# Attention in pairs of row blocks: which pair of blocks each iteration's 16 units begin with

## The chip, the cores and the metric

The kernel runs on one core of a Trainium2 chip, as a single program. The metric is the device time of that core in microseconds: the median of three runs is 3832.74 (3829.89 to 3833.71). A profiled execution, from which the rows below are taken, took 3835.85, and its span from first to last instruction is 3833.9.

## The reference

One transformer layer in float32 on x of 4 x 1024 x 512: layer norm, causal attention with 4 groups of 4 heads of width 128 (one key and value head per group), layer norm and residual; then a mixture of experts (32 experts, 4 per token, and a shared one) in the same frame.

```python
q = jnp.einsum('bim,ghmd->bghid', x, w_aq)
k = jnp.einsum('bim,gmd->bgid', x, w_ak)
v = jnp.einsum('bim,gmd->bgid', x, w_av)
q = _rope(q); k = _rope(k)
s = jnp.einsum('bghid,bgjd->bghij', q * qk_mult, k * qk_mult)
s = s - INF_APPROX * (i < j)
p = jax.nn.softmax(s, axis=-1)
o = jnp.einsum('bghij,bgjd->bghid', p, v)
r = jnp.einsum('bghid,ghdm->bim', o, w_ao)
...
x = x + _layernorm(attn(_layernorm(x)))
x = x + _layernorm(ffn(_layernorm(x)))
```

## The kernel before

Attention is a loop of 16 iterations, one for each batch b and group g, and it is written by hand for each engine: every engine has its own list, and they meet at semaphores. Numbers are kept as a high and a low part (names end in h and l), so each product is three matmuls (`mm3`, L820 to L822). One iteration has these stages.

Projection (`project`, tiles t = 0 to 7 of 128 rows): TensorE writes q, k and v of a tile into S, ScalarE copies it out (L726), VectorE and GpSimd do the rotation, TensorE turns the tile (`transpose_tile`, L862 for q and L865 for k), ScalarE casts the high part (`hi_tile`, L718 and L720) and VectorE subtracts to get the low part (`lo_tile`, L527 and L530).

Attention proper: the 8 row tiles form 4 row blocks of two tiles. A unit is one row block ib and one head h. With two row tiles a = 0 and 1 it has score blocks of (2 ib + 1) x 128 and (2 ib + 2) x 128 columns: 128 and 256 for block 0, 384 and 512 for block 1, 640 and 768 for block 2, 896 and 1024 for block 3. A unit has ib + 1 pairs of key tiles. BLOCKS says which two row blocks alternate in the first eight units and which in the last eight; UNITS, PAIRS, PROJECT_AT, OUTPUTS, PROJECTED and FINAL follow from it (L54 to L105). The steps of unit u are: scores (`scores`, two units ahead, into S[:, a]; the last piece adds the mask, L893), row maximum on VectorE (`row_max`, L559), exponential on ScalarE (`exp`, L734, which also frees S), transposes of the probabilities (`transpose_pair`, L908, into one of two banks of TP), the high part on ScalarE (`hi_pair`, L742) and the low part on VectorE (`lo_pair`, L571), the value matmuls (`value_pair`, which for a unit's first pair also spreads the reciprocals, L916), then L788, L577, L424 and L426, which normalise and split the result on ScalarE, VectorE and GpSimd. TensorE's list for a unit is, pair by pair: the transposes of the next pair, a score block of unit u + 2 for each of the first two pairs (a unit of block 0 has only one pair, and its second score block comes behind that), the value matmuls of this pair.

A transposes-ahead order means that the transposes of the pair after this one are issued first. When the next pair belongs to the next unit, they wait for both of that unit's exponentials. In `scores`, the first four units also wait for the low parts of the tiles they use: units 0 and 1 for tile i = 2 ib + a, unit 2 on for tile 7.

Output projection (`out_project`, L943 on): the first four row tiles at the start of units 8 and 9 (PROJECT_AT), the other four at the end (PROJECT_LAST).

Side work (`beside`), fixed to unit numbers by tables at L66 to L74: two portions of other tokens' norms, residual sum, transposes and router logits. The first has its steps at units 0, 1, 2, 2, 3, 3, 4, 6, 8 (XN, XH, XT_AT and RS, RA and RN, RH, HT_AT, LG_AT), the second at 8, 9, 9, 10, 10, 11, 12, 14, 15. On ScalarE these are L748, L751, L761, L764, L755 and L758, on VectorE L611, L600, L616, L622 with L624 and L625, L629 and L604 on, on GpSimd L362 to L383, on TensorE L959 and L964. The upper half of S[:, 1] is their transposes' target, and the second score block three units on waits until it has been read. GpSimd splits the weights for the next iteration and the output projection at odd units, and at unit 12 in three of the iterations it starts the reload of xTh and xTl (L409).

Of the kernel before, what the change touches and what calls it, by code (L numbers as in the profile page):

```python
# [50 lines left out]

IB = 2
NIB = NT // IB
BLOCKS = [(a, NIB - 1 - a) for a in reversed(range(NIB // 2))]  # L54
UNITS = [(ib, h) for blocks in BLOCKS for h in range(H) for ib in blocks]
PAIRS = [(u, jp) for u, (ib, h) in enumerate(UNITS) for jp in range(ib + 1)]
NPAIR = len(PAIRS)
# [39 lines left out]

PROJECT_AT = {HALFU + n: [IB * BLOCKS[0][n] + a for a in range(IB)] for n in range(2)}
PROJECT_LAST = [IB * ib + a for ib in BLOCKS[1] for a in range(IB)]

# [2094 lines left out]
```

## Time and profile before

| | |
|---|---|
| median of three runs | 3832.74 us |
| profiled execution | 3835.85 us, span 3833.9 us |
| TensorE busy | 3427.0 us, 89% |
| VectorE busy | 2253.4 us, 59% |
| GpSimd busy | 1635.9 us, 43% |
| ScalarE busy | 1603.6 us, 42% |
| attention, 16 iterations | about 38 to 2580 us |

A row of the timeline has the start, the time, the engine (PE is TensorE, DVE VectorE, ACT ScalarE, POOL GpSimd), the line of the kernel, the operation, output <- input by name, the shapes, the number merged into the row and, in brackets, how long the engine was idle before it and who released it. Times of a matmul row overlap with the next row's, as matmuls are pipelined. The iteration that begins at 514.97 is the one read closely.

### The profile page before, as it was taken

Reading aid. Unit: us, or ns where it says so; the run is one execution under the profiler, and the core shown is the slowest. Engines: PE = TensorE matmul, PEld = TensorE weight load, DVE = VectorE, ACT = ScalarE, POOL = GpSimd, SP = SyncE. Lnnn points to the kernel's source line nnn. Section 1 sums busy time; section 2 is a strip of 40 time slices with the busy share of each in tenths; the row PEclk is TensorE's granted clock in tenths of the full one; section 3 lists DMA queues with packets and bytes.
Section 4 is the critical chain, followed back from the end, with each engine's and each line's share of the span. In section 5 each row is a group of like instructions: output and inputs, shape, how many; then the busy total and the mean of one; then the engine's idle time right before and its main releaser. Section 6 shows DMA issues by size and latency. Waiting matters only on the chain. (4 is left out here: it accounts for less than half of the span.)

```text
span 3833.9 us, 73808 instructions
## 1 busy us (share of the span) xinstructions
PE 3427.0 (89%) x20373; PEld 2903.6 (76%) x20375; DVE 2253.4 (59%) x4900; ACT 1603.6 (42%) x3576; POOL 1635.9 (43%) x2112
## 2 busy tenths in 40 slices
PE   6999999999999999999899998985898999999987
PEld 5788777887878878778777787874686777777766
DVE  6665665656556565565665656655664454444448
ACT  2543534435344353443534435443123454444443
POOL 3433334333343333433334333345422555555548
PEclk9999999999999999999999999996899999999989
DMA  2111112111021210111121101126333777767767
GB/s 82 59 31 40 40 34 100 62 35 48 26 62 34 101 51 25 60 34 35 51 97 55 39 29 51 35 69 229 96 108 102 172 181 159 192 156 180 170 140 277
DMA packets 231764, 339.78 MB, mean 89 GB/s; under 512 B 20304, under 2 KB 105552, under 8 KB 230640
## 3 DMA queue, kind: packets, MB, share of 16 engines
q1 hardware_dynamic: 198128, 244.43, 19.7%
q0 software_dynamic: 33280, 91.02, 11.3%
q8 instruction: 173, 2.83, 0.3%
q14 instruction: 183, 1.50, 0.1%
HBM read 225.00 MB, written 110.38 MB: 87 GB/s over the span
## 5 line engine op out<-in xcount | busy, mean ns | idle before, releaser
L571 DVE TENSOR_TENSOR ptl<-TP,pth 128x512 fp32r<-128x512 f32 (+1 forms) x640 | 406.4, 635 | 231.3 <-ACT pth L742 223.7
L820 PE MATMUL O<-pth,vh 128*128 128x256 f32 (+1 forms) x1280 | 401.1, 313 | 55.9 <-DVE ptl L571 55.9
L742 ACT CAST pth<-TP 128x512 fp32r<-128x512 f32 (+1 forms) x640 | 344.5, 547 | 217.6 <-PE TP L908 216.4
L559 DVE TENSOR_REDUCE negmax<-S 128x1 f32<-128x384 f32 (+7 forms) x512 | 379.4, 748 | 27.2 <-PE S L893 25.3
L820 PE MATMUL S<-kTh,qTh 128*128 128x512 f32 (+3 forms) x768 | 302.5, 394 | 87.2 <-ACT work L734 40.1
L822 PE MATMUL O<-pth,vl 128*128 128x256 f32 (+1 forms) x1280 | 359.3, 281 | 0.0
L821 PE MATMUL O<-ptl,vh 128*128 128x256 f32 (+1 forms) x1280 | 358.6, 280 | 0.0
L820 PE MATMUL S<-wph,xTh 128*128 128x512 f32 (+1 forms) x1024 | 354.2, 346 | 3.5 <-issue 1.7
L402 POOL TENSOR_TENSOR work<-work,cst 128x320 f32<-128x320 f32 x128 | 132.3, 1034 | 504.8 <-ACT work L726 504.8
L821 PE MATMUL S<-wpl,xTh 128*128 128x512 f32 (+1 forms) x1024 | 346.6, 338 | 0.0
L822 PE MATMUL S<-wph,xTl 128*128 128x512 f32 (+1 forms) x1024 | 345.3, 337 | 0.0
L734 ACT ACTIVATE prob<-S,negmax 128x768 f32<-128x768 f32 (+5 forms) x288 | 265.5, 922 | 178.8 <-DVE negmax L559 178.8
L1651 POOL DMA_INDIRECT acc_d<-yb,idy x144 | 229.3, 1592 | 255.5 <-ACT yb L1702 238.5
L726 ACT COPY work<-S 128x768 f32<-128x768 f32 x128 | 102.5, 801 | 541.8 <-PE S L822 437.0
L820 PEld LDWEIGHTS O<-pth,vh 128*128 128x128 f32 x1280 | 243.2, 190 | 80.9 <-DVE ptl L571 80.5
L908 PE MATMUL TP<-cst,prob 128*128 128x128 f32 x1776 | 275.6, 276 | 17.9 <-ACT prob L734 17.7
L822 PE MATMUL S<-kTh,qTl 128*128 128x512 f32 (+3 forms) x768 | 268.2, 349 | 0.0
L821 PE MATMUL S<-kTl,qTh 128*128 128x512 f32 (+3 forms) x768 | 267.2, 348 | 0.0
L734 ACT ACTIVATE work<-S,negmax 128x128 f32<-128x128 f32 (+1 forms) x224 | 115.2, 514 | 333.5 <-DVE negmax L559 333.5
L1017 PE MATMUL S<-weh,hTh 128*128 (+1 forms) x576 | 242.9, 422 | 2.7 <-DVE wel L1741 2.7
L1034 POOL DMA_INDIRECT xg<-h_d,idx x146 | 192.9, 1321 | 122.2 <-DVE hTl L1749 54.7
L821 PEld LDWEIGHTS O<-ptl,vh 128*128 128x128 f32 x1280 | 243.2, 190 | 0.0
(319 smaller groups left out, 9341.8 us busy)
## 6 DMA issues: line engine op xcount, KB each, us to landing
raww<-in_L_ffn_w_dram SPq DMA_DIRECT2D x33, 1024.0 KB, 7.8
stage<-in_L_attn_w_aq_dram SPq DMA_DIRECT2D x68, 256.0 KB, 2.9
raww<-in_L_ffn_w_dram SPq DMA_DIRECT2D x33, 512.0 KB, 11.2
stage<-in_L_attn_w_ao_dram SPq DMA_DIRECT2D x64, 256.0 KB, 2.6
work<-in_L_attn_x_dram SPq DMA_DIRECT2D x64, 256.0 KB, 2.8
xt_d<-work SPq DMA_DIRECT2D x64, 256.0 KB, 3.0
a<-acc_d SPq DMA_DIRECT2D x64, 256.0 KB, 3.9
h_d<-work SPq DMA_DIRECT2D x40, 256.0 KB, 3.0
```

Source lines behind the costliest of these rows:

```text
L402: nc.gpsimd.tensor_tensor(dst[:, :, 0, :], src[:, :, 1, :], tab, ALU.mult)
L559: nc.vector.tensor_reduce(negmax[:, n % 4:n % 4 + 1], S[:, a, 0:(IB * ib + a + 1) * P], AX_X, ALU.max, negate=True).then_inc(max_ready, 1)
L571: nc.vector.tensor_tensor(ptl[:, n % 2, 0:w], TP[:, n % 2, 0:w], pth[:, n % 2, 0:w].bitcast(F32), ALU.subtract).then_inc(tp_lo, 1)
L734: nc.scalar.activation(probs(u, a)[:, 0:w], S[:, a, 0:w], ACT.Exp, bias=negmax[:, n % 4:n % 4 + 1], accum_out=rsum[:, n % 4:n % 4 + 1]).th ...
L742: nc.scalar.copy(pth[:, n % 2, 0:w], TP[:, n % 2, 0:w]).then_inc(tp_hi, 1)
L820: mm(out, ah, bh, start=first, stop=False)
L821: mm(out, ah, bl, start=False, stop=False)
L822: return mm(out, al, bh, start=False, stop=last)
L908: ins = nc.tensor.transpose(TP[:, n % 2, m * P:(m + 1) * P], probs(u, a)[:, j * P:(j + 1) * P], ident)
L1017: nc.tensor.matmul(out, ah, bh, start=first, stop=False)
L1034: nc.gpsimd.indirect_dma_start(xg[:, s], None, h_d, bass.IndirectOffsetOnAxis(ap=idx[:, s:s + 1], axis=0)).then_inc(landed[s], 16)
L1651: nc.gpsimd.indirect_dma_start(acc_d[s], bass.IndirectOffsetOnAxis(ap=idy[:, s:s + 1], axis=0), yb[:, s], None, compute_op=ALU.add).then_i ...
```

## The change

The two pairs of row blocks change places. BLOCKS was [(1, 2), (0, 3)] and is [(0, 3), (1, 2)]: the first eight units of every iteration alternate between blocks 0 and 3, the last eight between blocks 1 and 2. All tables that follow from it change with it: at units 8 and 9 the row tiles 0, 1 and 6, 7 are projected, at the end 2 to 5, and the last stage takes the tiles in that order. The side work keeps its unit numbers.

```diff
--- before.py
+++ after.py
@@ -51,7 +51,7 @@
 
 IB = 2
 NIB = NT // IB
-BLOCKS = [(a, NIB - 1 - a) for a in reversed(range(NIB // 2))]
+BLOCKS = [(a, NIB - 1 - a) for a in range(NIB // 2)]
 UNITS = [(ib, h) for blocks in BLOCKS for h in range(H) for ib in blocks]
 PAIRS = [(u, jp) for u, (ib, h) in enumerate(UNITS) for jp in range(ib + 1)]
 NPAIR = len(PAIRS)
```

The first place is the front: TensorE's list from the transposes of pair 0 of unit 0 on (L908, work or prob are the probabilities). Before:

```order
L905 REGISTER_ALU [waits s_read]
L908 MATMUL TP<-cst,prob 128x128 [waits tp_lo]
L908 MATMUL TP<-cst,prob 128x128 x3
L905 REGISTER_ALU
L908 MATMUL TP<-cst,prob 128x128 [waits tp_lo]
L908 MATMUL TP<-cst,prob 128x128 x2
L881 REGISTER_ALU [waits tp_lo]
L820 MATMUL S<-kTh,qTh 128x384 [waits s_read]
L821 MATMUL S<-kTl,qTh 128x384
L822 MATMUL S<-kTh,qTl 128x384
L893 MATMUL S<-mskb,idb 128x128
L922 REGISTER_ALU
```

Now:

```order
L905 REGISTER_ALU [waits s_read]
L908 MATMUL TP<-cst,prob 128x128 [waits tp_lo]
L908 MATMUL TP<-cst,prob 128x128 x2
L904 REGISTER_ALU
L908 MATMUL TP<-cst,prob 128x128 [waits tp_lo,s_read]
L908 MATMUL TP<-cst,prob 128x128 x3
L881 REGISTER_ALU [waits tp_lo]
L820 MATMUL S<-kTh,qTh 128x128 [waits s_read]
L821 MATMUL S<-kTl,qTh 128x128
L822 MATMUL S<-kTh,qTl 128x128
L893 MATMUL S<-mskb,idb 128x128
L922 REGISTER_ALU
```

The transposes of four blocks that wait for s_read (unit 1's exponentials) have moved ahead of unit 2's first score block (S<-kTh,qTh) and of unit 0's value matmuls (L924, L913).

The second place is the seam in the middle: TensorE's list from the last pairs of unit 7 to the output projections (L939 on). Before:

```order
L908 MATMUL TP<-cst,work 128x128 x2
L922 REGISTER_ALU
L820 MATMUL O<-pth,vh 128x256 [waits tp_lo]
L821 MATMUL O<-ptl,vh 128x256
L822 MATMUL O<-pth,vl 128x256
L820 MATMUL O<-pth,vh 128x128
L821 MATMUL O<-ptl,vh 128x128
L822 MATMUL O<-pth,vl 128x128
L904 REGISTER_ALU
L908 MATMUL TP<-cst,prob 128x128 [waits tp_lo,s_read]
L908 MATMUL TP<-cst,prob 128x128 x3
L939 REGISTER_ALU
```

Now:

```order
L908 MATMUL TP<-cst,work 128x128 [waits tp_lo,s_read]
L908 MATMUL TP<-cst,work 128x128 x3
L922 REGISTER_ALU
L820 MATMUL O<-pth,vh 128x256 [waits tp_lo]
L821 MATMUL O<-ptl,vh 128x256
L822 MATMUL O<-pth,vl 128x256
L820 MATMUL O<-pth,vh 128x128
L821 MATMUL O<-ptl,vh 128x128
L822 MATMUL O<-pth,vl 128x128
L908 MATMUL TP<-cst,work 128x128 [waits tp_lo]
L908 MATMUL TP<-cst,work 128x128 x2
L939 REGISTER_ALU
```

Before, the transposes that wait for s_read just ahead of the projections are those of unit 9; now these come later, and the wait for s_read in this piece is that of unit 8.

The third place is ScalarE's side work at unit 10: the copy of the side tile (L751) and the norm (L761). Before:

```order
L742 CAST pth<-TP 128x512 [waits pv_done,tp_done]
L733 REGISTER_ALU
L734 ACTIVATE work,rsum<-S,negmax 128x128 [waits max_ready]
L750 REGISTER_ALU
L751 CAST work<-S 128x512 [waits xp_done]
L760 REGISTER_ALU
L761 ACTIVATE work<-work,scr 128x512 [waits scr_ready]
L786 REGISTER_ALU
L787 REGISTER_ALU [waits pv_done]
L788 COPY onorm<-O 128x256 [waits o_split]
L733 REGISTER_ALU
L734 ACTIVATE work,rsum<-S,negmax 128x256 [waits max_ready]
```

Now:

```order
L742 CAST pth<-TP 128x384 [waits pv_done,tp_done]
L733 REGISTER_ALU
L734 ACTIVATE work,rsum<-S,negmax 128x384 [waits max_ready]
L740 REGISTER_ALU
L741 REGISTER_ALU [waits tp_done]
L742 CAST pth<-TP 128x512 [waits pv_done]
L733 REGISTER_ALU
L734 ACTIVATE work,rsum<-S,negmax 128x512 [waits max_ready]
L750 REGISTER_ALU
L751 CAST work<-S 128x512 [waits xp_done]
L760 REGISTER_ALU
L761 ACTIVATE work<-work,scr 128x512 [waits scr_ready]
```

In the unit of block 1 the second exponential (512 columns) and a second cast stand ahead of the copy, where in the unit of block 0 the second exponential (256 columns) stands behind it.

## Rows read from the trace of the kernel before

**Rows 1.** Timeline, TensorE, the first instruction of three iterations.

```profile
514.97 0.39 PE L820 MATMUL S<-wph,xTh 128*128 128x512 f32 x1
...
673.53 0.49 PE L820 MATMUL S<-wph,xTh 128*128 128x512 f32 x1 [0.27 <-issue]
...
832.70 0.49 PE L820 MATMUL S<-wph,xTh 128*128 128x512 f32 x1 [0.23 <-issue]
```

**Rows 2.** Waits of TensorE, 514 to 673: us, times, longest.

```profile
PE O L820 <- DVE ptl L571: 3.5, 7, 1.0
PE S L820 <- ACT work L734: 2.5, 3, 1.3
```

**Rows 3.** Timeline, TensorE, the front of the iteration.

```profile
553.60 0.66 PE L862 MATMUL TP<-cst,work 128*128 128x128 f32 x4 [1.04 <-DVE qTl L527]
...
556.54 0.50 PE L820 MATMUL S<-kTh,qTh 128*128 128x512 f32 x1 [1.41 <-ACT prob L734]
...
559.35 0.51 PE L820 MATMUL S<-kTh,qTh 128*128 128x512 f32 x1 [0.84 <-ACT prob L734]
...
562.80 0.43 PE L916 MATMUL O<-cst,rinv 128*128 128x128 f32 x2 [0.66 <-DVE ptl L571]
```

**Rows 4.** Timeline, VectorE, low part of tile 6's keys.

```profile
557.61 0.28 DVE L530 TENSOR_TENSOR kTl<-TP,kTh 128x128 fp32r<-128x128 f32 x1
```

**Rows 5.** Timeline, TensorE, a score block of 896 columns and what follows.

```profile
632.97 0.50 PE L820 MATMUL S<-kTh,qTh 128*128 128x512 f32 x1 [0.17 <-ACT work L734]
...
634.37 0.38 PE L916 MATMUL O<-cst,rinv 128*128 128x128 f32 x2
```

**Rows 6.** Timeline, VectorE, row maxima of 896 and 1024 columns.

```profile
603.52 1.08 DVE L559 TENSOR_REDUCE negmax<-S 128x1 f32<-128x896 f32 x1
...
604.99 1.21 DVE L559 TENSOR_REDUCE negmax<-S 128x1 f32<-128x1024 f32 x1
```

**Rows 7.** Timeline, ScalarE, unit 9's second exponential.

```profile
606.27 1.12 ACT L734 ACTIVATE prob<-S,negmax 128x1024 f32<-128x1024 f32 x1
```

**Rows 8.** Timeline, TensorE, unit 9's first transposes.

```profile
607.53 0.66 PE L908 MATMUL TP<-cst,prob 128*128 128x128 f32 x4 [1.10 <-ACT prob L734]
```

**Rows 9.** Timeline, TensorE, waits beside the first portion of side work.

```profile
579.71 0.47 PE L820 MATMUL S<-kTh,qTh 128*128 128x512 f32 x1 [0.99 <-DVE work L600]
...
581.45 0.39 PE L820 MATMUL O<-pth,vh 128*128 128x256 f32 x1 [0.39 <-DVE ptl L571]
...
587.80 0.39 PE L820 MATMUL O<-pth,vh 128*128 128x256 f32 x1 [0.94 <-DVE ptl L571]
...
594.06 0.38 PE L820 MATMUL O<-pth,vh 128*128 128x256 f32 x1 [0.98 <-DVE ptl L571]
```

**Rows 10.** Timeline, TensorE, waits beside the second portion of side work.

```profile
644.66 0.50 PE L820 MATMUL S<-kTh,qTh 128*128 128x512 f32 x1 [1.34 <-ACT work L734]
...
648.59 0.50 PE L820 MATMUL S<-kTh,qTh 128*128 128x512 f32 x1 [1.00 <-ACT work L734]
```

**Rows 11.** Timeline, VectorE, the residual sum of the first portion.

```profile
585.22 0.69 DVE L622 TENSOR_TENSOR work<-work 128x512 f32<-128x512 f32 x1 [0.80 <-ACT work L761]
```

**Rows 12.** Timeline, TensorE, waits at units 6, 14 and 15.

```profile
597.11 0.43 PE L916 MATMUL O<-cst,rinv 128*128 128x128 f32 x2 [0.23 <-DVE rinv L565]
...
654.88 0.43 PE L916 MATMUL O<-cst,rinv 128*128 128x128 f32 x2 [0.47 <-DVE rinv L565]
...
661.38 0.39 PE L820 MATMUL O<-pth,vh 128*128 128x256 f32 x1 [0.53 <-DVE ptl L571]
```

**Rows 13.** DMA issues, 640 to 680: KB each, us to landing.

```profile
xTl<-xt_d POOLq DMA_DIRECT2D x1, 2048.0 KB, 14.6
```

**Rows 14.** Busy by stretch: length, PE, PEld, DVE, ACT, POOL, then clock, DMA.

```profile
551.00:567.00 16.00, 12.05 (x84) 10.00 (x82) 11.63 (x27) 8.17 (x21) 1.69 (x2) 1.00 0.11 34
...
715.10:718.40 3.30, 3.19 (x13) 2.90 (x14) 2.46 (x5) 1.48 (x5) 0.00 (x0) 0.50 0.00 0
...
1027.00:1043.00 16.00, 13.00 (x70) 10.89 (x69) 10.49 (x22) 7.75 (x20) 1.68 (x2) 0.79 0.12 34
```

## The prediction

> **What bounds the kernel now.** I read the profile from the outside in. The 40 slices come first: TensorE is at 8 or 9 tenths in all of them, so its own order of work is the clock of the whole program. The attention part is 16 iterations that look alike; one starts at 514.97, the next at 673.53 and the one after at 832.70 [rows 1], so 158.56 and 159.17 us. Then I asked who waits for whom on TensorE inside one of them, 514 to 673 [rows 2]. The reader is to see that the waits are short (1.4 us at the longest) and come in small numbers from each source, and that they are for ScalarE and VectorE, not for DMA: TensorE is the bound, and the change can only move these gaps. It adds and removes no instruction. Each half of an iteration has eight units, four of the one kind and four of the other, and both halves have 20 pairs and 40 score and value blocks in either order. So the question is what each gap depends on: on the kind of unit (then it moves along), on the seam between two stages (then it changes), or on the side work, which is tied to unit numbers.
>
> **The front, where projection turns into attention.** Now units 0 and 1 are of blocks 1 and 2, and TensorE waits 1.04, 1.41, 0.84 and 0.66 us there [rows 3], 3.95 in all. Afterwards they are of blocks 0 and 3, and four things follow, in order of the instructions.
> (a) The first score block is 128 wide in place of 384. TensorE is through some 0.24 us earlier, and the next wait, for tile 5, ends where it did: 1.04 becomes 1.28.
> (b) The first score block of unit 1 is row block 6 in place of 4. It needs the keys of tile 6, whose low half VectorE ends at 557.61 + 0.28 = 557.89 [rows 4]. VectorE starts that tile when ScalarE has cast the high half, and ScalarE does this behind the first exponential; with 128 columns both that and the row maximum are shorter, some 0.5 us together, so the keys are there at about 557.4. TensorE is done with the second score block (256 wide, 0.35 us shorter) at 554.8. Wait: 2.65 in place of 1.41.
> (c) This block is 896 wide (1.40 us from start to next instruction, 632.97 to 634.37 [rows 5]), so it ends at 558.9, tile 7's transposes at 559.6. The last score block, row block 7, needs tile 7's keys. VectorE's queue has the row maximum of the 896 columns (1.08 [rows 6]) ahead of that tile, so it is at 561.1. Wait: 1.5 in place of 0.84.
> (d) A unit of block 0 has a single pair. So behind the transposes of pair (0,0) stand those of unit 1, which need both its exponentials, where now there is one more pair of unit 0 and a score block between. The chain from the end of the last score block is the maximum of 1024 columns, 1.21 [rows 6], and their exponential: 606.27 to TensorE's restart at 607.53, 1.26 [rows 7, 8]. 562.9 + 1.21 + 1.26 = 565.4; TensorE is idle from 563.15. Wait: 2.25 in place of 0.66. The value blocks of unit 0 come behind it and find everything ready.
> Sum of the front: 7.7 against 3.95, +3.75 an iteration. Bounds: +2.5, if the first exponential's shortening reaches tile 7 too; +5, if the backlog also delays the scores of units 2 and 3.
>
> **The seam in the middle.** Today TensorE waits 1.10 us at the start of unit 8 for the exponential of unit 9 [rows 8]: unit 7 is of block 2 and unit 8 a short one. Afterwards unit 7 is of block 3, with a pair more, and unit 8 (block 1) has a pair of its own and two output projections ahead of unit 9's transposes. −1.10. Bounds −1.10 and −0.6.
>
> **The side work** (norms, transposes and logits of other tokens) is tied to unit numbers: first portion in the first half, second in the second. Its gaps while blocks 1 and 2 run are 0.99, 0.39, 0.94 and 0.98 [rows 9]; while blocks 0 and 3 run, 0.17, 1.34 and 1.00 [rows 5, 10]. Most belong to the kind of unit and move along: 0.99 is the wait for the side tile behind an exponential that in a unit of block 1 stands ahead of its copy, 0.98 the multiply at L629, and 1.34 and 1.00 are the GpSimd chain between L625 and L764, for which a unit of block 0 is too short. What doesn't is the spacing: the first portion has its statistics at unit 2 and both norm and sum at unit 3, where VectorE waits 0.80 for ScalarE's norm [rows 11] and delivers the next pair late (0.94). The second portion has them at 9, 10 and 11. Placed on blocks 1 and 2 it has neither the 0.9 us of statistics behind the side copy (0.39) nor the wait of 0.80: −0.39 − 0.94 = −1.33. The first portion on blocks 0 and 3 has its norm at the end of a long unit, where ScalarE is ready before VectorE, and loses the 0.17. Together −1.4; bounds 0 (the waits only move to the next pair) and −3.3 (all four go).
>
> **The end of an iteration.** Units 14 and 15 have no scores ahead of them to fill with: 0.47 for a reciprocal and 0.53 for the last pair, besides 0.23 at unit 6 [rows 12]. With blocks 1 and 2 there the reciprocal gap is 0.23 plus the missing score block, about 0.6, the next 0.1, and the last pair is covered by the logits and one pair. Unit 6 is then covered by wider scores. 0.7 in place of 1.23: −0.5. Bounds −1.2 and +0.7. The output projections of the last four tiles wait for GpSimd's splits of units 14 and 15; 4 us of unit 15 lie over the first and 5.6 us of projections over the second, so nothing comes there.
> SyncE's queue and GpSimd's splits are issued at odd units, and two neighbouring units are five pairs in either order, so their stages come when they did. The one to watch is the reload of xTh and xTl at unit 12 in three iterations, which lands 14.6 us after its issue [rows 13]. By the pattern of the first half its issue stands some 18.5 us ahead of the next projection, in place of 21: hidden, with 3 us to spare. The tiles' order in the last stage changes too; their number doesn't, and I cost it at nothing.
>
> **The clock.** At the front's gaps the granted clock falls to half (1.2 of 2.4 GHz) for about 3.4 us in 6 of 16 iterations: it is 1.00 over the front of one of the others, 0.50 right behind the gap of 1.41 in a single fall, and 0.79 over the front of the iteration with a double fall [rows 14]. An iteration with a fall is 159.17 [rows 1], the nine without are 158.2 to 158.6 (leaving out the first), the double one is 159.9. So a fall costs about 0.85. With the gaps nearly doubled I expect one in each iteration, and a second in about half, since there are two large gaps, (b) and (d), apart from each other: (16 + 8) x 0.85 = 20 less the present 6 = +15 us over the program. Bounds: 0 and 16 x 2 x 1.7 (what half clock takes from 3.4 us of dense work) = 54.
> The Trainium skill ("TensorE: Matmul & The Clock Gate", section "HAM oscillation — how this bites in real kernels") says that a wait which recurs in every tile lets the clock fall in every tile, and then the work behind it pays. That speaks against this change. Today's trace agrees only in part, with 6 of 16; by the rule alone, one fall in each of 16, the clock's term would be 14 − 6 = +8.
>
> **Sum.** 3.75 − 1.10 − 1.4 − 0.5 = +0.75 an iteration, x 16 = +12, and the clock +15: +27 us. The profiled execution took 3835.85 (span 3833.9), so 3862.9 for such a one; the median shown, 3832.74, is 3.1 lower, and I take 3860.
>
> **The rivals.**
> 1. The falls are free: they lie on gaps in which TensorE waits anyway, as today's partly does. For it: an iteration with a fall loses the wait of 0.84. Against: it is still 0.8 longer. Time 3833 + 12 = 3845 (with part of the front's low bound, 3835).
> 2. Faster: the side work is what counts. Its gaps on blocks 1 and 2 all go when its steps are spread over units 9 to 12, because VectorE, which delivers the pairs, is never late: −3.3 in place of −1.4, and the end empties too (−1.2): +3.75 − 1.10 − 3.3 − 1.2 = −1.85, x 16 = −30, 3803 without the clock, 3818 with its term, which is the rival's time. It decides from the point where side work and end together give back over 3.6 us an iteration with the clock's term. Against: two of the four gaps have causes that I find in the kind of unit.
> 3. Slower by more: VectorE's and ScalarE's waits in the side work only move to the next pair (0 in place of −1.4), +22 us: 3882. For it: a pair's two casts follow each other closely everywhere.
> 4. Nothing moves: the gaps belong to the kinds of unit and the front is hidden. Against: the wait for tiles 6 and 7 is written in the program. I count it with the first.
>
> **Chances.** Forecast 0.36 (own range 3848 to 3872), first with fourth 0.26, second 0.20, third 0.18. The range for 8 in 10 is 3812 to 3888. What can be told from no change is 0.2%, 3825 to 3840: the second lies below it, with 0.02 of the first, and 0.16 of the first and 0.02 of the forecast's lower edge lie in it. Faster 0.22, same 0.18, slower 0.60.
>
> **What would show it.** In the profile of the changed kernel, at the front of an iteration: waits of about 1.3, 2.7, 1.5 and 2.3 us on TensorE, the second for kTl (L530) and the fourth for an exponential of 1024. No wait for an exponential at the start of unit 8. No wait of 0.80 at L622 in the second half, and none on L820 for L571 behind it. Granted clock below 1.00 at the front of all iterations. An iteration would be about 160 us. I am wrong if the front's waits sum below 6, or if the iterations are shorter than 158.4.

## The result, and the profile after

The changed kernel takes 3911.89 us (median of four runs, 3906.95 to 3917.47) against 3831.49 (3829.89 to 3833.71) beside it: a ratio of 1.021 [1.0191, 1.0229], 80 us slower, where 3860 was forecast. Its profiled execution took 3916.34. The page, the busy row and the slices:

```profile
span 3914.2 us, 73792 instructions
...
PE 3485.5 (89%) x20373; PEld 2947.0 (75%) x20375; DVE 2253.8 (58%) x4900; ACT 1607.0 (41%) x3576; POOL 1636.2 (42%) x2112
...
PEclk9999999999999999999999999996899999999999
```

VectorE, GpSimd and ScalarE are busy for as long as before, to within 4 us. TensorE has the same matmuls and is busy 58 us longer (3427.0 before). A busy time that grows without more work points to the clock; the slices are too coarse to show it. An iteration shows both halves of the loss, the waits and the clock. The timeline gives the starts of the first iteration, of the one read closely, of the next, and of the sixteenth:

```profile
38.74 0.79 PE L820 MATMUL S<-wph,xTh 128*128 128x512 f32 x1 [1.68 <-DVE xTl L511]
...
860.09 0.49 PE L820 MATMUL S<-wph,xTh 128*128 128x512 f32 x1
...
1024.26 0.49 PE L820 MATMUL S<-wph,xTh 128*128 128x512 f32 x1 [0.17 <-issue]
...
2499.28 0.46 PE L820 MATMUL S<-wph,xTh 128*128 128x512 f32 x1
```

(2499.28 − 38.74) / 15 = 164.04 us an iteration, against 158.89 before (37.94 to 2421.26, by the same two starts; [rows 1] show three others): +5.15, x 16 = +82, the whole difference. The expert part behind the attention is the same in both, to within 3 us.

The front of the iteration at 860.09, as TensorE's timeline has it, answers to [rows 3] and [rows 8]:

```profile
898.82 0.66 PE L862 MATMUL TP<-cst,work 128*128 128x128 f32 x4 [1.27 <-DVE qTl L527]
...
902.76 0.79 PE L820 MATMUL S<-kTh,qTh 128*128 128x512 f32 x1 [2.75 <-DVE kTl L530]
...
905.28 1.06 PE L862 MATMUL TP<-cst,work 128*128 128x128 f32 x4
...
908.02 0.79 PE L820 MATMUL S<-kTh,qTh 128*128 128x512 f32 x1 [1.46 <-DVE kTl L530]
...
910.86 0.85 PE L908 MATMUL TP<-cst,prob 128*128 128x128 f32 x3
...
913.62 0.66 PE L908 MATMUL TP<-cst,prob 128*128 128x128 f32 x4 [1.91 <-ACT prob L734]
```

The waits are those of the prediction, (a) to (d), in size (1.27, 2.75, 1.46, 1.91; the last is up to 2.2 in other iterations) and in source. What was not foreseen stands between them. The score block of 896 columns takes 905.28 − 902.76 = 2.52 us to the next instruction, where it took 1.40 before [rows 5], and the one of 1024 takes 2.84. The windows of after say why (length; busy us of TensorE, its weight loads, VectorE, ScalarE and GpSimd, with counts; granted clock; DMA share; GB/s):

```profile
243.00:265.00 22.00, 14.59 (x68) 11.88 (x69) 11.96 (x28) 7.91 (x22) 2.46 (x5) 0.69 0.09 25
...
572.00:594.00 22.00, 15.23 (x91) 12.33 (x92) 13.83 (x30) 8.94 (x23) 2.95 (x7) 0.84 0.09 25
...
901.60:902.70 1.10, 0.00 (x0) 0.00 (x0) 0.96 (x3) 0.27 (x2) 0.00 (x0) 0.50 0.00 0
...
902.00:912.00 10.00, 7.49 (x22) 5.20 (x22) 3.83 (x7) 2.57 (x7) 0.00 (x0) 0.51 0.19 52
912.00:915.20 3.20, 1.57 (x15) 1.58 (x16) 1.18 (x5) 2.02 (x4) 0.00 (x0) 0.99 0.00 0
915.40:918.70 3.30, 3.30 (x14) 2.92 (x14) 2.54 (x9) 1.76 (x6) 0.47 (x2) 0.52 0.02 5
...
38.00:2662.00 2624.00, 2395.31 (x15228) 2075.81 (x15229) 1571.76 (x3392) 1109.19 (x2544) 986.49 (x1542) 0.96 0.15 48
```

The first two are the same 22 us of the front in two other iterations. Over these 22 us the clock is 0.69 or 0.70 in twelve of the sixteen iterations, 0.61 in one and 0.84 in three. In the iteration at 860.09 it goes to half (1.2 GHz) within wait (b), of which the last 1.1 us are shown, and stays there for some 10 us, over both large score blocks and the wait (c) between them; it comes back for 3 us, and falls once more over 3.3 us in which TensorE is busy without a gap (3.30 of 3.30). Before, there was one fall in 6 of 16 iterations, of about 3.4 us in five of them and of 6.8 in the sixth. This is that longest one of before, and its whole attention part:

```profile
1032.70:1039.20 6.50, 6.28 (x24) 5.62 (x25) 4.27 (x8) 3.13 (x10) 0.00 (x0) 0.50 0.23 61
...
38.00:2580.00 2542.00, 2339.33 (x15232) 2034.15 (x15232) 1568.96 (x3391) 1105.10 (x2544) 986.27 (x1542) 1.00 0.16 49
```

Over the attention part the mean clock went from 1.00 to 0.96, and TensorE's busy time from 2339 to 2395 us, with the same work. At 1.2 GHz it spends 24 us of it before and 201 us after.

The waits of TensorE in this iteration answer to [rows 2] (in total, times, longest):

```profile
PE S L820 <- DVE kTl L530: 4.2, 2, 2.7
PE S L820 <- ACT work L734: 2.4, 2, 1.5
PE TP L908 <- ACT prob L734: 1.9, 1, 1.9
PE O L820 <- DVE ptl L571: 1.4, 3, 1.0
PE TP L862 <- DVE qTl L527: 1.3, 1, 1.3
PE S L820 <- DVE work L600: 1.0, 1, 1.0
PE O L916 <- DVE rinv L565: 0.6, 1, 0.6
PE O L820 <- DVE onorm L577: 0.3, 1, 0.3
```

The reader is to see that VectorE's ptl fell from 3.5 (seven times) to 1.4 (three times), that the seam's wait for an exponential is gone (the one left on L908 is (d)), and that the sum hardly grew. I call the waits that the timeline marks, which are those of 0.15 us and more, labelled waits; an ordinary iteration is one without the reload of xTh and xTl and not the first. Over the ordinary iterations all labelled waits make 13.5 us in the median, and 12.8 in an iteration of before without a fall. By these waits alone the change would cost 11 us.

### The profile page after: what moved, and what is told of

The parts are those of the page before. It is cut to its first block and busy times, and to the rows that moved or that the text cites. A ratio compares the mean times of both kernels' runs of the same rounds, so it can differ in the third digit from the quotient of the medians.

```text
span 3914.2 us, 73792 instructions
## 1 busy us (share of the span) xinstructions
PE 3485.5 (89%) x20373; PEld 2947.0 (75%) x20375; DVE 2253.8 (58%) x4900; ACT 1607.0 (41%) x3576; POOL 1636.2 (42%) x2112
## 5 line engine op out<-in xcount | busy, mean ns | idle before, releaser
L571 DVE TENSOR_TENSOR ptl<-TP,pth 128x512 fp32r<-128x512 f32 (+1 forms) x640 | 405.8, 634 | 275.9 <-ACT pth L742 268.8
L559 DVE TENSOR_REDUCE negmax<-S 128x1 f32<-128x128 f32 (+7 forms) x512 | 380.1, 748 | 123.5 <-PE S L893 123.0
L820 PE MATMUL S<-kTh,qTh 128*128 128x512 f32 (+3 forms) x768 | 317.9, 414 | 123.5 <-DVE kTl L530 68.1
L734 ACT ACTIVATE prob<-S,negmax 128x1024 f32<-128x1024 f32 (+5 forms) x288 | 258.6, 898 | 132.8 <-DVE negmax L559 132.4
L908 PE MATMUL TP<-cst,prob 128*128 128x128 f32 x1712 | 274.7, 280 | 34.2 <-ACT prob L734 34.2
L822 PE MATMUL S<-kTh,qTl 128*128 128x512 f32 (+3 forms) x768 | 282.1, 367 | 0.0
L821 PE MATMUL S<-kTl,qTh 128*128 128x512 f32 (+3 forms) x768 | 280.7, 365 | 0.0
L820 PEld LDWEIGHTS S<-kTh,qTh 128*128 128x128 f32 x768 | 155.5, 202 | 160.1 <-issue 95.7
L734 ACT ACTIVATE work<-S,negmax 128x384 f32<-128x384 f32 (+1 forms) x224 | 122.3, 546 | 327.4 <-DVE negmax L559 327.4
L822 PEld LDWEIGHTS O<-pth,vl 128*128 128x128 f32 x1280 | 246.0, 192 | 0.0
```

The costliest lines, as they stand in the source:

```text
L559: nc.vector.tensor_reduce(negmax[:, n % 4:n % 4 + 1], S[:, a, 0:(IB * ib + a + 1) * P], AX_X, ALU.max, negate=True).then_inc(max_ready, 1)
L571: nc.vector.tensor_tensor(ptl[:, n % 2, 0:w], TP[:, n % 2, 0:w], pth[:, n % 2, 0:w].bitcast(F32), ALU.subtract).then_inc(tp_lo, 1)
L734: nc.scalar.activation(probs(u, a)[:, 0:w], S[:, a, 0:w], ACT.Exp, bias=negmax[:, n % 4:n % 4 + 1], accum_out=rsum[:, n % 4:n % 4 + 1]).th ...
L820: mm(out, ah, bh, start=first, stop=False)
L821: mm(out, ah, bl, start=False, stop=False)
L822: return mm(out, al, bh, start=False, stop=last)
```

## The experiments

My theory after the result: the front's waits, longer now, let the clock fall in each iteration, and the falls are most of the 80 us. The rival: the falls come along with the waits and cost little, as before, and the time is lost in waits that bear no label. To keep the clock up without touching any order, I put matmuls whose result nobody uses into TensorE's list, ahead of the four waits. They write to the second output bank, O[:, 1], and the `wait_ge` ahead of them sees that it is free. They are of 512 columns and take 0.25 us each (11 take 2.78), so they end about when the awaited part comes. Ratios below are to the kernel before as it ran beside each experiment: 3835.57 us beside e1 to e4, 3837.03 beside e5 to e7 and 3839.11 beside e8 and e9.

```diff
+def fill(n):
+
+    for _ in range(n):
+        mm(O[:, 1], xTh[:, 0, 0:P], wph[:, 0, 0:QW], start=True, stop=True)
+
+pe.wait_ge(o_free, m0 + 2)
...
 scores(0, 0)
+fill(4)
 transpose_tile(NT - 2)
 scores(0, 1)
+fill(11)
 scores(1, 0)
 transpose_tile(NT - 1)
+fill(5)
 scores(1, 1)
...
         n = PAIR_OF[(u, jp)] + 1
+        if n == 1:
+            fill(8)
         if n < NPAIR:
             transpose_pair(n)
```

**e1_after_filled**, the changed kernel with 4, 11, 5, 8 such matmuls.

> The changed kernel with matmuls added whose result nobody uses: 4, 11, 5 and 8 of 512 columns ahead of the four waits at the front of each iteration (0.9, 2.4, 1.1 and 1.7 us at full clock, less than the waits of 1.27, 2.75, 1.46 and 2.1), so that TensorE is busy while it waits. Theory A: of the 80 us, some 12 are longer waits and the rest is the granted clock, which falls for 10.2 and 3.4 us in every iteration. Filled, the clock stays at 1.00 over the front, and the time is 3838 to 3850. Rival B: the 80 us are in the waits and what hangs on them, and the falls lie on time that is lost anyway: 3900 to 3915, more if the added matmuls delay what stands behind them.

**e2_before_filled**, the kernel before with 3, 5, 2, 2; the last two stand ahead of unit 0's value matmuls, where this kernel has its fourth gap.

> The kernel before with the same kind of added matmuls, 3, 5, 2 and 2, ahead of its four waits at the front (1.04, 1.41, 0.84 and 0.66). Theory A: the falls in 6 of 16 iterations go, 3824 to 3828, and the difference to the filled changed kernel is that of the waits alone, about 12 us. Rival B: its falls cost nothing, 3831 or a little more, and the changed kernel filled stays 70 us or more above it.

Measured: e1 3857.03, ratio 1.0054 [1.0037, 1.0071]; e2 3831.91, ratio 0.9989 [0.9978, 1.0]. e1's windows, a front and then the whole attention part:

```profile
878.00:900.00 22.00, 20.65 (x126) 16.34 (x125) 14.73 (x31) 10.04 (x27) 3.73 (x7) 1.00 0.07 25
...
38.00:2600.00 2562.00, 2434.78 (x15677) 2096.51 (x15678) 1573.03 (x3392) 1107.15 (x2544) 987.06 (x1542) 1.00 0.15 49
```

and its timeline over the front, beside the one of after above:

```profile
883.00 0.49 PE L820 MATMUL S<-kTh,qTh 128*128 128x512 f32 x1 [0.18 <-DVE kTl L530]
...
884.39 0.61 PE L862 MATMUL TP<-cst,work 128*128 128x128 f32 x4
...
886.67 0.49 PE L820 MATMUL S<-kTh,qTh 128*128 128x512 f32 x1 [0.42 <-DVE kTl L530]
...
888.23 0.50 PE L908 MATMUL TP<-cst,prob 128*128 128x128 f32 x3
```

There is no fall left in the attention part of either, and the changed kernel has lost three quarters of its 80 us with 448 matmuls more in it. It is still above the 3838 to 3850 expected of it, since the waits cost more than the expected 12 us. From the start of row block 6's scores to the end of row block 7's it is 888.23 − 883.00 = 5.23 us here and 910.86 − 902.76 = 8.10 in after: 2.87 us of each iteration lie in that one chain. An iteration of e1 is (2441.09 − 38.42) / 15 = 160.18, one of e2 (2416.94 − 37.51) / 15 = 158.63. So the rival is refuted, and the 80 us split by ratios of 3832: the waits are e1 less e2, 1.0054 / 0.9989 = 1.0065, 25 us; the falls of after are 80.4 − 20.7 = 60; the falls of before were 4. By the intervals each of these is good to some 8 us; the iterations' lengths give the same split, 16 x (160.18 − 158.63) = 25, 16 x (164.04 − 160.18) = 62 and 16 x (158.89 − 158.63) = 4.

**e3_after_filled_ab** (4, 11, 0, 0) and **e4_after_filled_d** (0, 0, 0, 8): which wait draws which fall.

> The changed kernel with only the first two of its four front waits filled (4 and 11 matmuls), so that the wait of 1.46 and that of 2.1 us stay empty. Theory A1: the long fall is drawn by the waits of 1.27 and 2.75 and goes, and with it the stretching of the chain from the scores of row block 6 to those of row block 7, 2.9 us an iteration; a fall of 3.4 us in dense work behind the last wait stays: 3840 + 16 x 1.7 = 3867. Rival A2: any two of the waits suffice for the long fall: 3890 or more.

> The changed kernel with only the last of its four front waits filled (8 matmuls ahead of the transposes of unit 1). Theory A1: the long fall of 10.2 us stays and stretches the chain, the short one of 3.4 us behind it goes: 3911 - 27 = 3884. Rival A2: both falls come from the waits of 1.27 and 2.75 us: 3905 to 3915. By rival B no change or more.

Measured: e3 3870.11, 1.0094 [1.0075, 1.0113]; e4 3890.83, 1.015 [1.013, 1.0169]. Windows of e3 over two fronts:

```profile
76.00:98.00 22.00, 17.73 (x105) 14.72 (x104) 13.29 (x31) 9.05 (x23) 3.02 (x6) 0.92 0.08 25
...
881.00:903.00 22.00, 17.67 (x113) 14.11 (x111) 14.89 (x31) 10.06 (x27) 3.58 (x7) 1.00 0.08 25
```

Five of its 16 fronts are at 0.92, with one fall of 3.4 us, the other eleven at 1.00. Windows of e4 over two:

```profile
238.00:260.00 22.00, 17.30 (x87) 13.84 (x88) 12.69 (x29) 8.29 (x22) 3.09 (x7) 0.77 0.08 25
...
401.00:423.00 22.00, 16.99 (x99) 13.80 (x100) 13.88 (x30) 8.93 (x23) 2.92 (x6) 0.92 0.08 25
```

Nine at 0.77 (the long fall of 10 us), seven at 0.92 (a short one); the second fall, in the dense work, is gone in all. So the long fall goes when (a) and (b) are filled (which of the two it needs was not tested), and the second fall goes when (d) is. Filling ahead of (a) and (b) alone gives back 44 us of the 60 (1.021 to 1.0094). Both times are near the ones expected with these falls, 3867 and 3884. Counts of falls, here and below, are from one profiled execution of each kernel.

**e7_after_half_filled** (2, 5, 2, 4): must the waits be filled, and what do the added matmuls cost?

> The changed kernel with about half of each front wait filled: 2, 5, 2 and 4 matmuls, so that some 4.8 us of the 7.7 stay empty, somewhat more than the 3.95 of the kernel before. Theory A: how much the clock costs goes by how empty the front is; with the emptiness near that of before the falls are near those of before too (single ones of 3.4 us in some to all iterations): 3855 to 3872. Rival C: any wait longer than those of before draws the long fall: 3895 or more.

Measured: 3861.06, 1.0067 [1.0052, 1.0081], the same as e1 within the intervals. Its waits between 839 and 999, the three of the front:

```profile
PE S L820 <- DVE kTl L530: 2.7, 2, 1.5
...
PE TP L908 <- ACT prob L734: 1.3, 1, 1.3
...
PE TP L862 <- DVE qTl L527: 0.8, 1, 0.8
```

its timeline at (c) and (d), and its attention part as one window:

```profile
883.73 0.27 PE L865 MATMUL TP<-cst,work 128*128 128x128 f32 x1
...
885.57 0.49 PE L820 MATMUL S<-kTh,qTh 128*128 128x512 f32 x1 [1.11 <-DVE kTl L530]
...
887.13 0.50 PE L908 MATMUL TP<-cst,prob 128*128 128x128 f32 x3
...
889.85 0.66 PE L908 MATMUL TP<-cst,prob 128*128 128x128 f32 x4 [1.29 <-ACT prob L734]
...
38.00:2600.00 2562.00, 2379.08 (x15439) 2050.98 (x15438) 1571.77 (x3391) 1106.88 (x2543) 986.71 (x1542) 1.00 0.15 49
```

Gaps of 0.76, 1.54, 1.11 and 1.29 us are left, and the clock doesn't fall once. In the iteration shown, each instruction behind the front stands as far from the iteration's start as in e1, to 0.06 us (0.17 at most in the others), although 15 matmuls an iteration are gone: the added work costs nothing, and e1 shows the true price of the waits. The expectation had single falls in some to all iterations; its time, 3855 to 3872, came out without them. The rows also give (c) and (d) as they are at full clock, with the added matmuls taken as idle time: 885.57 − 884.00 = 1.57 and 889.85 − 887.63 = 2.22.

**e6_before_seam** and **e5_before_filled_seam** (with 3, 5, 2, 2 besides) test the prediction's second step by itself: in the kernel before, the wait of 1.10 at unit 8 [rows 8] can be covered by putting the two output projections ahead of unit 9's transposes, as the change does in passing.

```diff
+ahead8 = u == HALFU and jp == 0
+for t in PROJECT_AT.get(u, []) if ahead8 else []:
+    out_project(t)
 if n < NPAIR:
     transpose_pair(n)
...
-for t in PROJECT_AT.get(u, []) if jp == 0 else []:
+for t in PROJECT_AT.get(u, []) if jp == 0 and not ahead8 else []:
     out_project(t)
```

> The kernel before, its front waits filled as in the earlier filled kernel (3, 5, 2 and 2 added matmuls), and at unit 8 the two output projections put ahead of the transposes of unit 9's first pair, so that 5.6 us of matmuls cover the exponential for which TensorE waits 1.10 there. Theory: the seam's 1.10 us is a term of its own, worth 16 x 1.1 = 18 us: 3810, a ratio of 0.994. Rival: the wait only moves to the value matmuls of unit 9, whose pair is now cast later: 3827, a ratio of 0.999.

> The kernel before with only the two output projections of unit 8 put ahead of the transposes of unit 9's first pair, nothing filled. Theory: 3832 - 18 = 3814, and the granted clock falls at the front of some iterations as before. Rival: no change, 3832.

Measured: e5 3869.61, 1.0085 [1.0069, 1.0101]; e6 3879.89, 1.0115 [1.01, 1.0129]. Both slower: the expectation failed. TensorE's timeline of e6 has, in place of the 1.10:

```profile
1268.52 0.43 PE L916 MATMUL O<-cst,rinv 128*128 128x128 f32 x2 [1.83 <-DVE racc L586]
```

and VectorE's, in an earlier iteration:

```profile
945.07 0.69 DVE L571 TENSOR_TENSOR ptl<-TP,pth 128x512 fp32r<-128x512 f32 x1 [4.83 <-ACT pth L742]
...
945.81 1.26 DVE L586 TENSOR_TENSOR racc<-racc,O 128x512 f32<-128x512 f32 x2
```

The projections hold both banks of O until VectorE adds them to racc (L586). VectorE's list has `lo_pair(9, 0)` ahead of that, and this needs unit 9's transposes, which now stand behind the projections: VectorE is idle 4.83 us, in most of which the first finished bank is there, and TensorE then waits 1.83 for one of them. The clock falls for 3.4 or 6.8 us behind this wait in 11 of 16 iterations, in e5 and in e6. The falls are most of the loss: an iteration of e5 is 159.1 us without a fall (158.4 in e2, and 1.83 − 1.10 = 0.73 is the longer wait), 160.8 with one of 3.4 us and 162.3 with one of 6.8. Two windows of e6:

```profile
780.00:796.00 16.00, 14.16 (x66) 12.09 (x65) 6.25 (x18) 2.54 (x8) 3.10 (x6) 0.79 0.11 34
...
942.00:958.00 16.00, 14.17 (x86) 12.12 (x85) 7.58 (x19) 2.65 (x9) 3.60 (x7) 1.00 0.11 34
```

**e8_before_filled_seam_dve** and **e9_before_seam_dve**, the same as e5 and e6, with VectorE's list in the matching order:

```diff
+if u == HALFU and jp == 0:
+    add_results(PROJECT_AT[u])
 if n < NPAIR:
     lo_pair(n)
...
-if jp == 0:
+if jp == 0 and u > HALFU:
     add_results(PROJECT_AT.get(u, []))
```

> As e5 (the kernel before, front filled, output projections of unit 8 ahead of unit 9's first transposes), and on VectorE the additions of unit 8's projection results ahead of the low part of unit 9's first pair. In e5 that low part stood first in VectorE's queue and held the additions back, so that the output bank came free late and TensorE waited 1.83 us on L586 in place of 1.10 on the exponential. Theory: with the additions first both waits are gone, 158.6 becomes 157.5 us an iteration, 3832 - 4 - 18 = 3810, ratio 0.9945. Rival: a third wait at units 8 and 9 takes the place, no faster than 3827.

> As e8 without the added matmuls at the front. Theory: the seam's wait is worth 18 us without them too, and the clock falls at the front of some iterations as in the kernel before (some 4 us): 3814. Rival: with another length of the iteration the falls come in more iterations than before, up to all 16, and take back up to 16 x 0.85 = 14 us: 3825.

Measured: e8 3810.58, 0.9925 [0.9911, 0.994]; e9 3811.11, 0.9931 [0.9917, 0.9946]. Both are faster than the kernel before, by 0.7%, near the 3810 and 3814 expected, and the best versions found. e8's waits between 840 and 1000 (its lines from L612 on are numbered two higher):

```profile
PE O L822 <- DVE ptl L571: 3.5, 7, 1.0
PE S L822 <- ACT work L736: 2.5, 3, 1.3
...
PE O L918 <- DVE rinv L565: 0.7, 2, 0.5
PE S L822 <- ACT prob L736: 0.6, 2, 0.4
```

Neither the wait for an exponential at unit 8 nor the one of 1.83 is there, and an iteration is (2399.59 − 38.33) / 15 = 157.42, against 158.63 in e2: 1.21 less: the seam's 1.10 was worth its full length. e9, without added matmuls, has three falls in the whole attention part, where before had one in each of six iterations; that a shorter seam would draw more of them was not borne out.

## Why the prediction was wrong in size

The direction and the places of the waits came out; the size didn't, as the time (3912) lies above the range's end (3888). The step that failed is the clock's term, below. The signs that the prediction named for being wrong did not come: the front's waits sum to 7.4, and an iteration is 164.04 long, where about 160 was forecast and e1, without falls, has 160.18.

**The front, (a) to (d): right.** Forecast 1.28, 2.65, 1.5, 2.25; measured 1.27, 2.75, 1.46 and 1.9 to 2.2, and at full clock (e7) 1.57 and 2.22 for the last two. The sources are the ones named, kTl of tiles 6 and 7 (L530) and the exponential of 1024.

**The middle seam: right, with a small new wait.** The 1.10 [rows 8] is gone. At the start of unit 9's work TensorE now waits 0.32 for unit 8's output bank (O <- onorm L577 in the waits above), which I had not seen. e5 and e6 show that the gain hung on something the prediction named only in passing: unit 8, of block 1, has a pair of its own, whose transposes stand ahead of the projections, so VectorE's next entry is not held by them. Why the changed kernel escapes this is read from the order of the lists, not tested.

**The side work and the end: right.** 0.39, 0.94 and 0.17 of [rows 5, 9] are gone; 0.99, 0.98, 1.34 and 1.00 [rows 9, 10] stay as 1.01, 0.98, 1.46 and 0.98: −1.4, as forecast, with some luck. The prediction's own items, −1.33 and −0.17, make −1.5, and the 1.34 grew by 0.12, for which it had nothing. The end has 0.6 for a reciprocal and little else in place of 1.23 [rows 12].

**The waits' sum: +12 forecast, +25 measured.** The labelled waits of after rise by 0.7 an iteration, 11 us, which is near the forecast, but the half clock had shortened (c) and (d). At full clock an ordinary iteration is 1.45 longer (159.85 in e1 and 158.40 in e2, medians of the ordinary ones). With the added matmuls taken as idle time, the labelled waits of such an iteration are 13.70 in e1 and 12.78 in e2: +0.92 where +0.75 was forecast, 15 us. Seven or eight waits of under 0.15 us, for the low parts (L571), reciprocals (L565) and one exponential, most of them in the second half, come to 0.53 where e2 has two of 0.07 together: +0.46, 7 us, a term that the prediction put at nothing. TensorE's busy time is the same to 0.13. In the three iterations with the reload of xTh and xTl the difference is 0.7 more than that, 2 us in all: the part that I dismissed with 3 us to spare. By e1's trace GpSimd issues the two transfers (L409, 0.81 and 0.60 us) ahead of unit 12's split, ScalarE waits for that split, and the last pairs come late to TensorE, which waits 1.06 for ptl at 664.32. That was read, not tested. The landing, which I had watched, is hidden.

**The clock: the step that failed.** "So a fall costs about 0.85 … (16 + 8) x 0.85 = 20 less the present 6 = +15 us over the program." It is 60 − 4, so about +56, about the bound of 54 that I had given and left out of the range. The number of falls was forecast well enough (one in each iteration, and a second in 14 of 16 where I had half). Two things were wrong in their price.
First, the length. I took 3.4 us for each, and called the longer fall of before [rows 14] a double one, where it is a single fall of 6.8 us, in an iteration 1.4 longer than those without. Now the first lasts 10 us in twelve of the iterations. The end of (b) and the whole of (c) stand under it, with 3.8 us of work between them (902.76 to 906.56, where (c) begins). With (a) and (b) filled no fall is longer than 3.4 us (e3); with (d) alone filled nine still are (e4). That (c) prolongs what (b) begins is how I read this; no run filled (c) alone.
Second, what lies under it. Before, a fall of 3.4 us lay partly over the wait of 0.84: TensorE was slower but had to wait anyway, and 0.85 was left. Now the fall lies over row block 6's and row block 7's scores, and these are on the chain: tile 7's transposes stand behind the first, its keys and (c) behind these, and (c) hardly shrinks (1.46 for 1.57) while the block ahead of it grows by 1.12: from the start of row block 6's scores to that of row block 7's it is 908.02 − 902.76 = 5.26 us, and 886.67 − 883.00 = 3.67 in e1. 8.10 against 5.23 us, +2.87. The second fall lies in dense work, where nothing hides anything: at the transposes of unit 1 after is 2.88 us behind e1 in the iteration and at the next labelled wait (935.01 − 860.09 = 74.92, against 911.08 − 840.30 = 70.78) 4.14. The difference, 1.26, is its price; in e5 a fall of 3.4 us in dense work cost 1.7 and one of 6.8 cost 3.2. 4.1 us together: my 0.85 was the price of neither.
The Trainium skill ("TensorE: Matmul & The Clock Gate", section "HAM oscillation — how this bites in real kernels") holds that a wait recurring in every tile brings the clock down in every tile. The trace of after agrees, with all 16 fronts below 1.00; one fall an iteration at my 0.85 would have been +8. That section of the Trainium skill takes half of the throttled time as the penalty; from the 201 us at 1.2 GHz that makes an estimate of 100 us. The runs gave 60, and the measurement decides. In the long fall read here some 2.7 of the 10 us are waits, the end of (b) and the whole of (c), and neither is longer than at full clock in e7.

**The rivals.** The first (falls are free) is refuted by e1. The third came nearest in time, 3882, by a mechanism that did not occur: the side work's waits did not move to the next pair. The second has its place half right, VectorE's ptl waits do go from 3.5 to 1.4, but two of its four gaps stayed (1.01 and 0.98). The slices that I read first are not 8 or 9 in all: the page has a 6 at the start, a 5 just behind the attention and a 7 at the end; no term rests on that.

## What to carry to other kernels

Before pricing a fall of the clock from a trace in which it is rare, look at what lies under it. A fall of 3.4 us cost 0.85 here where it lay partly over a wait and 1.3 to 1.7 over dense work; one of 10 us over a chain of dependent work and its waits cost 2.9. Don't take its length from the rare ones either: with longer gaps it was three times as long in most iterations. When a change makes the waits of the busiest engine longer in each iteration, try once with useless matmuls ahead of them: it separates the wait from the clock in one run. When work is moved on one engine, move its consumer's entry in the other engine's list as well; half a move cost 1.2%, the whole one gained 0.7%.

## What the runs showed of the hardware

The sum of the idle time does not tell whether the clock falls. Gaps of 1.04, 1.41, 0.84 and 0.66 us, 3.95 in all, drew one fall, of 3.4 us and once of 6.8, in 6 of 16 iterations; 0.76, 1.54, 1.11 and 1.29 (e7), 4.70 in all, with matmuls ahead of each, drew none; one gap of 1.83 amid work (e6) drew one of 3.4 or 6.8 us in 11 of 16; and 1.27, 2.75, 1.46 and 1.9 to 2.2 drew 10 us at 0.51 in most of the iterations, and a further 3.3 us at 0.52 in work without any gap. That further one was gone in all 16 iterations when the gap of 1.9 to 2.2 ahead of it was filled (e4). A fall can thus show behind its cause, over work that is as dense as can be.
